# Attention on one Trainium2 core: from single heads in hi/lo halves to pairs of heads on halves of the array in plain float32

## What is computed

```python
xn = _layernorm(x, axis=-1)
x = x + gnn(xn, W1, b1, W2, b2, eps, src, dst) + mix(xn[None], W_qkv, W_out, b_out)[0]
x = x + ffn(_layernorm(x)[None], ...)[0]

# mix: HEADS = 8, DIM_HEAD = 64
q = q * SCALE
qk = jnp.einsum('bhnd,bhmd->bhnm', q, k)
qk = jax.nn.relu(qk)
attn = jnp.einsum('bhnm,bhmd->bhnd', qk, v)
out = attn.transpose(0, 2, 1, 3).reshape(B, N, HEADS * DIM_HEAD)
return jnp.einsum('bne,de->bnd', out, W_out) + b_out
```

## Time and profile before

| | us |
|---|---|
| median of 3 runs | 882.88 (881.28 to 884.25) |
| the profiled execution | 883.28 |
| its span, first to last instruction | 881.5 |
| projections of v, 102.0 to 149.2 | 47.2 |
| attention with graph work, 149.2 to 508.2 | 359.0 |
| output projection, 508.2 to 542.7 | 34.5 |

### The profile page before, as it was taken

How to read it: one execution, slowest core, us unless ns; L and a number is a source line. 1 busy time by engine, 2 the same in 40 slices (tenths; PEclk the granted TensorE clock), 3 DMA queues, 4 the chain that set the end, 5 groups by cost and what they waited for, 6 DMA issues and landing times.

```text
span 881.5 us, 11457 instructions
## 1 busy us (share of the span) xinstructions
PE 773.4 (88%) x3351; PEld 517.5 (59%) x3352; DVE 519.3 (59%) x1488; ACT 280.9 (32%) x575; POOL 154.5 (18%) x198
## 2 busy tenths in 40 slices
PE   1999998998989998989799999999998599999910
PEld 1555543665756665666577744677887256766700
DVE  6444345797989899888977535434445533333224
ACT  1311111352525443434345401323333123434400
POOL 5040002112040304040400043002021100000044
PEclk9999999998999999989899999999999559999965
DMA  9016000807153435344261081001015945343357
GB/s 301 2 41 242 1 0 1 293 2 237 59 165 131 140 145 160 134 124 172 65 230 48 1 336 67 1 0 63 10 73 191 365 183 197 108 139 111 129 167 229
DMA packets 47015, 111.61 MB, mean 127 GB/s; under 512 B 7034, under 2 KB 7050, under 8 KB 44528
## 3 DMA queue, kind: packets, MB, share of 16 engines
q1 hardware_dynamic: 42192, 91.41, 30.6%
q0 software_dynamic: 3616, 11.17, 4.0%
q10 hardware_dynamic: 1152, 8.39, 2.4%
HBM read 44.73 MB, written 58.54 MB: 117 GB/s over the span
## 4 chain that ended last, share of the span: by engine, by line
PE 72%; DVE 18%; issue 4%; POOL 2%; DMA 2%; ACT 1%; DVEq 0%; POOLq 0%; SPq 0%
PE bank L1082 9%; PE bank L1104 8%; PE bank L1234 7%; PE bank L1180 6%; PE bank L1295 6%; PE bank L1131 6%; PE bank L1308 5%; DVE arena L797 5%; DVE p_lo L833 5%; PE bank L1053 4%; PE bank L1114 4%; PE bank L1165 4%; PE bank L1150 4%; PE bank L1147 3%; DVE arena L799 3%
## 5 line engine op out<-in xcount | busy, mean ns | idle before, releaser
L630 ACT ACTIVATE p_hi<-bank 128x416 fp32r<-128x416 f32 (+1 forms) x240 | 124.0, 519 | 201.6 <-PE bank L1131 200.2
L833 DVE SCALAR_TENSOR_TENSOR p_lo<-bank,p_hi 128x416 fp32r<-128x416 f32 (+1 forms) x240 | 140.2, 586 | 40.8 <-ACT p_hi L630 39.7
L797 DVE TENSOR_SCALAR arena<-iota,arena 125x128 f16<-125x128 f16 x392 | 135.5, 346 | 42.0 <-PE bank L1053 39.8
L799 DVE TENSOR_SCALAR arena<-iota,arena 125x320 f16<-125x320 f16 x392 | 115.8, 295 | 0.0
L1131 PE MATMUL bank<-q_hi,k_hl 128*128 128x416 f32 (+1 forms) x240 | 114.6, 478 | 0.1
L1150 PE MATMUL bank<-p_lo,v_hl 128*128 128x416 f32 (+1 forms) x240 | 90.8, 378 | 22.4 <-DVE p_lo L833 22.0
L1082 PE MATMUL bank<-arena 128*128 128x512 f32 x200 | 103.9, 601 | 0.8 <-ACT arena L597 0.8
L1053 PE MATMUL bank<-arena 125*128 125x320 f16 x392 | 95.8, 309 | 5.1 <-issue 4.0
L1147 PE MATMUL bank<-p_hi,v_hl 128*128 128x416 f32 (+1 forms) x240 | 86.5, 360 | 0.0
L1131 PE MATMUL bank<-q_lo,k_hl 128*128 128x416 f32 (+1 forms) x240 | 86.1, 359 | 0.0
L1053 PEld LDWEIGHTS bank<-arena 125*128 125x128 f16 x392 | 34.4, 99 | 74.5 <-issue 53.8
(11 more groups left out here) (208 smaller groups left out, 1019.4 us busy)
## 6 DMA issues: line engine op xcount, KB each, us to landing
slots<-arena SPq DMA_DIRECT2D x6, 5376.0 KB, 19.1
slots<-arena SPq DMA_DIRECT2D x2, 5120.0 KB, 19.1
arena<-in_ew SPq DMA_DIRECT2D x8, 1024.0 KB, 10.2
arena<-in_ew ACTq DMA_DIRECT2D x8, 1024.0 KB, 12.9
arena<-slots SPq DMA_DIRECT2D x32, 256.0 KB, 2.8
slots<-arena SPq DMA_DIRECT2D x28, 256.0 KB, 2.0
arena<-in_gw SPq DMA_DIRECT2D x2, 2048.0 KB, 17.0
arena<-in_wqkv SPq DMA_DIRECT2D x4, 768.0 KB, 16.5
```

The lines of the kernel that those rows point to most:

```text
L630: act.activation(p_hi[0:kt, s % NPB, 0:n], bank[s % NQB][0:kt, 0:n], ACT.Relu).then_inc(p_hi_ready, 1)
L797: dve.tensor_scalar(ring[:, at_slot:at_slot + P], iota16[0:CE, 0:P], window_cols[:, i % WBUF, 1, k:k + 1], None, ALU.is_equal)
L799: dve.tensor_scalar(ring[:, at_slot + P:at_slot + OHW], iota16[0:CE, :], window_cols[:, i % WBUF, 0, k:k + 1], None, ALU.is_equal).then_in ...
L833: dve.scalar_tensor_tensor(out=p_lo[0:kt, s % NPB, 0:n], in0=bank[s % NQB][0:kt, 0:n], scalar=0.0, in1=p_hi[0:kt, s % NPB, 0:n].bitcast(f3 ...
```

## The change

The attention's steps are now over pairs of heads: 4 pairs, 3 blocks, 10 tiles of keys, 120 steps. For a step PE makes two scores matmuls, one for each head of the pair, with 64 rows of contraction each, in the upper and in the lower half of the array's rows (`tile_position` (0, 0) and (64, 0)), into two banks. ACT takes the relu of one head, DVE of the other, and neither waits for the other. Then PE makes two values matmuls, each with 128 rows and 64 output columns, on the left and on the right half of the array's columns, into the two halves of one bank. All four are plain float32. With this go

- the hi/lo split on POOL, the three copies for each head on SP, `p_lo`, DVE's part of v, and the adding of halves;
- the reload of x, since v now takes half the room: POOL adds `xn` and the bias before the attention ends, and DVE's bias add (L846) goes;
- the loads of `w_o` and `w2` move to the first attention step; w1 still waits for the last. The eight fills are issued each 15 steps.

Scores run one step ahead in two sets of two banks, there are three probability buffers, one bank for the value sums. `EVERY` is 3.35, so that a step carries about three one-hot pairs instead of one and a half, and the neighbour sums stand two to a step.

```diff
-        NPB = 4
+        NPB = 3
-        k_hl = [split_tensor(f"k_hl{i}", b, [N]) for i, b in enumerate((SET0, SET1))]
-        q_hi = [split_tensor(f"q_hi{i}", b + 4 * N, [N]) for i, b in enumerate((SET0, SET1))]
...
+        probs = at(PROBS, [NPB, 2, BW])
+        v_sb = at(VT, [NT, D])
...
-        steps = [(h, b, t) for h in range(HEADS) for b in range(len(BLOCKS)) for t in range(NT)]
+        steps = [(p, b, t) for p in range(PAIRS) for b in range(len(BLOCKS)) for t in range(NT)]
-        EVERY = 6.7
+        EVERY = 3.35
...
-                    pe_after[made + 5 + t].append(("sum", g, t))
-                dve_after[made + NT + 6].append(("sum", g))
+                    pe_after[made + 4 + t // 2].append(("sum", g, t))
+                dve_after[made + 9].append(("sum", g))
...
-            sp.dma_start(xr[:, 0:9, :], xv).then_inc(x_again, 16)
...
             for t in range(NT):
                 link(pool.tensor_tensor(xr[:, t, :], xr[:, t, :], xn[:, t, :], ALU.add))
+                link(pool.tensor_tensor(xr[:, t, :], xr[:, t, :], bias_b2[:, :], ALU.add))
                 pool.sem_inc(base_ready, 1)
...
-                act.activation(p_hi[0:kt, s % NPB, 0:n], bank[s % NQB][0:kt, 0:n], ACT.Relu).then_inc(p_hi_ready, 1)
+                act.activation(probs[0:kt, s % NPB, 0, 0:n], bank[2 * (s % 2)][0:kt, 0:n],
+                               ACT.Relu).then_inc(p0_ready, 1)
...
-                dve.wait_ge(p_hi_ready, s + 1)
...
-                dve.scalar_tensor_tensor(out=p_lo[0:kt, s % NPB, 0:n], in0=bank[s % NQB][0:kt, 0:n], scalar=0.0,
-                                         in1=p_hi[0:kt, s % NPB, 0:n].bitcast(f32), op0=ALU.max,
-                                         op1=ALU.subtract).then_inc(p_lo_ready, 1)
+                dve.wait_ge(qk_ps, s + 1)
+                if s >= NPB:
+                    dve.wait_ge(av_step, s - NPB + 1)
+                dve.tensor_single_scalar(probs[0:kt, s % NPB, 1, 0:n], bank[2 * (s % 2) + 1][0:kt, 0:n], 0.0,
+                                         op=ALU.max).then_inc(p1_ready, 1)
...
-                for first, q in ((True, q_hi), (False, q_lo)):
-                    ins = pe.matmul(bank[s % NQB][0:kt, 0:n], k_hl[h % 2][:, t * P:t * P + kt], q[h % 2][:, o:o + n],
-                                    start=first, stop=not first)
+                for a in range(2):
+                    ins = pe.matmul(bank[2 * (s % 2) + a][0:kt, 0:n], k_t[DH * a:DH * a + DH, p, t * P:t * P + kt],
+                                    q_t[DH * a:DH * a + DH, p, o:o + n], start=True, stop=True,
+                                    tile_position=(DH * a, 0))
...
+                pe.wait_ge(p0_ready, s + 1)
+                pe.wait_ge(p1_ready, s + 1)
+                for a in range(2):
+                    h = 2 * p + a
+                    ins = pe.matmul(bank[AV][DH * a:DH * a + DH, 0:n], v_sb[0:kt, t, h * DH:h * DH + DH],
+                                    probs[0:kt, s % NPB, a, 0:n], start=(t == 0), stop=(t == NT - 1),
+                                    tile_position=(0, DH * a), skip_group_check=True)
+                ins.then_inc(av_step, 1)
```

More of the change, by code:

```diff
@@ L260, in layer @@
         neigh_ps, rst_ready, rstt_ps, rstt_saved = (sem(s) for s in ("neigh_ps", "rst_ready", "rstt_ps", "rstt_saved"))
[L261 to L265, removed]
+        qk_ps, p0_ready, p1_ready, av_step, av_saved = (
+            sem(s) for s in ("qk_ps", "p0_ready", "p1_ready", "av_step", "av_saved"))
+        v_saved = sem("v_saved")
         out_ps, out_added = sem("out_ps"), sem("out_added")
@@ L346, in _ @@
                          allow_slow_non_contiguous=True).then_inc(eb1_in, 16)
[L348 to L355 removed]
+            sp.wait_ge(zeros_ready, 1)
+            for i, fill in enumerate(FILLS):
+                sp.wait_ge(qk_ps, 1 + i * NS // len(FILLS))
                 sp.dma_start(xs[fill.start:fill.stop, :].rearrange("(t p) d -> p t d", p=P),
                              zeros.unsqueeze(1).to_broadcast([P, len(fill) // P, D])).then_inc(zero_filled, 16)
[L359 to L360 removed]
+                if i == 0:
+                    sp.dma_start(w_o[:, :, :], wo).then_inc(wo_in, 16)
+                    sp.dma_start(w2[:, :, :], gw2).then_inc(w2_in, 16)
             def expert(e):
@@ L534, in spare_window @@
                     pool.sem_inc(spare_waited, 1)
-            for _, what, i in sorted([(start(0) + 0.5 if h == 0 else NPRE + SPH * (h - 1) + 1, "head", h) for h in range(HEADS)]
-                                     + [(start(max(w - 2, 0)), "cols", w) for w in range(NW)]
+            for _, what, i in sorted([(start(max(w - 2, 0)), "cols", w) for w in range(NW)]
                                      + [(start(w), "spare", w) for w in range(0, NW, 2)]):
-                {"head": split_head, "cols": window_columns, "spare": spare_chunks}[what](i)
-            pool.wait_ge(av_step, NS)
-            link(pool.memset(xr[96:P, NT - 1, :], 0.0))
-            pool.sem_inc(xpad_ready, 1)
-            pool.wait_ge(x_again, 32)
+                {"cols": window_columns, "spare": spare_chunks}[what](i)
             for t in range(NT):
                 link(pool.tensor_tensor(xr[:, t, :], xr[:, t, :], xn[:, t, :], ALU.add))
+                link(pool.tensor_tensor(xr[:, t, :], xr[:, t, :], bias_b2[:, :], ALU.add))
                 pool.sem_inc(base_ready, 1)
@@ L1111, in _ @@
                 if t >= 5:
-                    pe.wait_ge(v_lo_ready, t - 4)
+                    pe.wait_ge(v_saved, t - 4)
                 for k in range(KD):
@@ L1142, in _ @@
                 m = s // NT
-                if t == 0 and m >= 2:
-                    pe.wait_ge(av_saved, m - 1)
-                pe.wait_ge(p_hi_ready, s + 1)
-                pe.matmul(bank[AV + m % 2][:, 0:n], v_hl[0:kt, t, h, :, :], p_hi[0:kt, s % NPB, 0:n],
-                          start=(t == 0), stop=False)
-                pe.wait_ge(p_lo_ready, s + 1)
-                pe.matmul(bank[AV + m % 2][:, 0:n], v_hl[0:kt, t, h, :, :], p_lo[0:kt, s % NPB, 0:n],
-                          start=False, stop=(t == NT - 1)).then_inc(av_step, 1)
+                if t == 0 and m >= 1:
+                    pe.wait_ge(av_saved, m)
+                pe.wait_ge(p0_ready, s + 1)
[6 more added lines that the diff above has]
+                ins.then_inc(av_step, 1)
                 graph(NPRE + s)
@@ L1158, in _ @@
                 r = rows(t)
-                pe.wait_ge(av_saved, SPH * HEADS // NT - len(BLOCKS)
-                           + sum(1 for o, n in BLOCKS if o < t * P + r))
+                pe.wait_ge(av_saved, NM - len(BLOCKS) + sum(1 for o, n in BLOCKS if o < t * P + r))
                 if t >= 8:
```

107 lines of the change are left out of this document (25 added, 82 removed).

## The result

The changed kernel takes 891.61 us (median, 889.5 to 893.17) against 882.69 us before: a ratio of 1.0097, 95% interval 1.0082 to 1.0113. It is slower, by 8.9 us and not by 59. Its profiled span is 890.1 us.

What follows compares the result with a forecast made beforehand. PE and DVE were taken as about level in the attention, waiting for each other. PE's 120 x (2.10 + 0.30) = 288 us plus 43, 78, 4 and 4 gave 418 us against 359.0, so 942 us; range 858 to 1040 us.

Steps and rivals of the forecast that it cites:

- How the two matmuls of a pair share the array: PE's attention step: only first head's second record and second head's first run together, three slots of 0.35 us, not four.
- The term of 120 x 2.10 us: PE's scores and values matmuls over 120 attention steps, 1.05 us for each two matmuls, 2.10 us a step.
- The changes of shape: PE's array goes from row halves to column halves to whole: three changes of 0.1 us, 0.3 us a step.
- The row taken as nearest: First float32r matmul after a float16 one on PE: next start after 0.30 us instead of 0.19, 0.1 us more.
- Rival 1: Attention pairs run wholly together on PE: 1.40 us a step plus changes, 858 us in all; chance 0.24.
- the point that decides: Attention keeps its 359 us at 1.91 us a step, so three changes may cost up to 0.5 us a step.
- PE for nearly nothing: Sign in the attention's timeline: DVE and ACT wait for PE, while PE itself waits for nearly nothing.
- The ring's loop: DVE's relu stands behind a one-hot pair waiting for one of six slots: 1.9 us against PE's 1.82, if changes are free.
- POOL's adds: 20 adds of 1.7 us, 34 us, starting some 45 us before the attention's end; hold-ups of one-hot instructions under 5 us.
- POOL loses its split: In the attention POOL's split and DVE's 35 us of stalls go, worth nothing since PE sets the pace.
- What bounded the kernel before: Attention of 359 us: PE 307 us and DVE some 295 about level; 52 us are waits and changes between matmul kinds.
- no lasting fall of the clock: Denies the rival that half-array matmuls leave PE's clock at 0.50, doubling the steps' 2.40 us: above 1200 us; chance 0.06.

Runs made afterwards that it cites:

- The run on the same half: Changed kernel with both heads' scores taken from the upper half of the partitions, so both matmuls use the same half of the array's rows: 971.9 us.
- The 12-slot kernel: Changed kernel with a ring of 12 one-hot slots instead of 6, order of work unchanged: 879.91 us, ratio 0.9976 against the kernel before.
- Giving the lumps back: Changed kernel with 12 one-hot slots, POOL doing the removed split's four instructions seven times into memory nobody reads: 897.62 us.

## Why the prediction was wrong in size and right in sign

- **How the two matmuls of a pair share the array: wrong, and the largest step.** "I take this one: all rows of plain float32 show two records one behind the other, and none shows an overtaking." In the order of their starts the records of the two heads are interleaved, so two slots do, not three. Whether the program has them in that order or one overtakes another, the trace doesn't say. The term of 120 x 2.10 us is 120 x 1.40, 84 us less. The rule of the Trainium skill (TensorE: Matmul & The Clock Gate, Part 3) that matmuls on different tiles overlap, some 4 ns apart, held for plain float32 too, with 5 to 7 ns between the first records; the prediction gave it the smaller chance. The run on the same half shows that the order it assumed costs what it said where the halves are the same.
- **The changes of shape: mechanism right, mis-sized.** 0.3 us a step was taken, within 0 to 0.8. It is 0.09 us at each of three entries, 0.10 and 0.05 us for the second records of scores and values, and another 0.10 us in the 45 steps in which a sum follows: about 0.47 us a step. The 12-slot kernel's stage nearly closes with it: 120 x 1.40 + 43 + 77 + 4 = 292 us, changes 120 x 0.47 = 56, waits 4: 352 of 354. The row taken as nearest doesn't show a price at all: there the first float32r matmul starts only 0.04 us behind the one-hot product, so that the 0.04 and 0.30 us are together the 0.14 + 0.19 us that they cost without a change. That 0.1 us came out for the entries is luck. That the second record's part is a weight load that can't be hidden behind a change is argued from its halving at 64 columns; no run changes it alone. The Trainium skill (TensorEngine Tiling (Array Packing), Key Properties) says that changing the tiling mode drains TensorE. What the starts show at the first record behind a change is 0.09 us; whether that is the drain, no run here shows.
- **Rival 1 is what happened**, with those terms: 292 + 56 + 14 us of waits + 2 for the clock = 364 us, and the stage measured 367.0. It says that the point that decides is 0.5 us of changes a step, without any waits. The changes came out at 0.47, and the waits put the time on the other side: with 12 slots the same order of work takes 879.9 us, less than before. So the sign was right by luck. "Slower" was forecast for a third slot that isn't there, and it came from waits that the forecast had at nothing ("PE for nearly nothing"). Rival 1's range was said to end at 918 us, so the measured time lay in it; but it was counted for faster in four fifths.
- **The ring's loop: right as a mechanism, wrongly left out.** It was priced only for changes that cost nothing. 12 slots gave 11.7 us, with changes at their full price. Even at that price the loop is the longer one, for it was undersized: 1.9 us stood there, and the lines of one turn, in the experiment with 12 slots, give 2.31 against PE's own 2.26.
- **POOL's adds: seen, and undersized.** "At most the few pairs left, under 5 us." They ran from 440 to 470 us, 77 to 47 us before the stage's end, with one-hot pairs still to make until 480. Their four large waits are 7 us, and the half clock behind them 1.6 us.
- **"POOL loses its split ... both are worth nothing here": wrong by some 18 us.** Giving the lumps back costs 17.7 us in the kernel with 12 slots, which PE bounds. For DVE's share alone it was right (60 us more, no difference).
- **What bounded the kernel before: right in the main.** 35 us of stalls in all were read, 26 for six of eight heads were expected, 27 came. But the 52 us between PE's load and the stage were put down to waits and changes of kind alone, and some 10 of them were the clock, at 0.50 for 23.9 us behind those waits (an estimate, worked out above). That 26 and 27 agree so closely is in part chance.
- **The rest held**: no gain from the reload of x, from `w2` and `w_o`, from the v stage; w1 in time; 373.3 us behind the stage in both; no lasting fall of the clock, which is at full speed for all but 3.4 us of the stage.

## What to carry to other kernels

Pairs of 64-row or 64-column matmuls ran fully side by side on halves of the array, in plain float32 too, but each change between shapes cost 0.1 to 0.2 us, so put as many matmuls of one shape in a row as banks and buffers allow. An engine with 40% to spare can still set the pace: look at which of its instructions is waited for, what stands right in front of it (a ring slot, a save, a long neighbour on POOL), and how many steps of slack it has. A wait can cost twice: look for the granted clock behind it. And price such a loop whenever a step is rebuilt, not only for the case in which the main engine has become fast.

## What the runs showed of the hardware that was not expected

- Plain float32 matmuls of one pair start within 0.01 us of each other, and their second records within 0.04 us; with no change of shape a pair of records costs 0.35 us for 416 columns, the same as one.
- Two matmuls on the same half are fully serial: 1.59 us for the four records instead of 0.90.
- Behind a change of shape the second record of a float32 matmul is late as well: 0.10 us for 128 columns of weights, 0.05 for 64.
- POOL instructions over 64x1250 values hold up a float16 one-hot instruction on DVE for up to their own length (2.85 us beside 2.95 us), in the kernel before and in the changed one with the load put back: 0.11 us on the mean of some 310. POOL's adds over 128x512 values do the same (1.31 us beside 1.26 us). The second instruction of a one-hot pair, over 125x320 values, kept its 0.30 us in the mean.
- The granted clock stood at 0.50 for 23.9 us of the attention before, behind such waits of PE, and for 3.4 us without most of the split.
